# Reordering the first two batches of a fused attention and layer-norm kernel

## What is computed

```
u = einsum('bld,bmd->blm', h, h) / sqrt(d)
p = softmax(u, axis=-1)
delta = p * adjacency
attn = delta / (sum(delta, axis=2) + 1e-10)
h_left, h_self, h_right = h @ W_left.T + b_left, h @ W_self.T + b_self, h @ W_right.T + b_right
attn_left  = where(j > i, attn, 0)      # above the diagonal
attn_right = where(j < i, attn, 0)      # below it
ctx = attn_left @ h_left + diag(attn) * h_self + attn_right @ h_right
o = layernorm(ctx, eps=1e-12) * gamma + beta
x = layernorm(x + relu(o), eps=1e-5)
```

## Times and profile before

| | us |
|---|---|
| median of 3 runs | 479.48 |
| lowest, highest | 479.28, 480.9 |
| the profiled execution | 482.81 |
| its span in the trace | 481.1 |
| PE busy, share | 464.3, 97% |
| DVE busy, share | 360.3, 75% |
| ACT busy, share | 325.8, 68% |
| POOL busy, share | 222.2, 46% |

### The profile page before, as it was taken

The page is one execution under the profiler, slowest core; times in us unless marked ns, Lnnn a source line. Parts: engine busy times, 40 slices in busy tenths (PEclk is TensorE's granted clock), DMA queues, the critical chain, the costliest instruction groups (busy, mean ns, idle before and its releaser), DMA issues.

```text
span 481.1 us, 9627 instructions
## 1 busy us (share of the span) xinstructions
PE 464.3 (97%) x2712; PEld 459.5 (96%) x2712; DVE 360.3 (75%) x1088; ACT 325.8 (68%) x715; POOL 222.2 (46%) x294
## 2 busy tenths in 40 slices
PE   8989799999999999999999999999999999999992
PEld 7979799999999999999999999999999999999982
DVE  5667667887777778877777887777788777777756
ACT  6644666677667667766766776676677667667752
POOL 0104543445554444555444455544445554444552
PEclk8999799999999999999999999999999999999998
DMA  8555465465565644556555455655445566544211
GB/s 254 161 162 186 146 187 190 128 194 181 184 188 185 200 138 163 184 176 198 185 172 159 166 183 170 207 185 173 153 165 185 174 207 185 170 156 134 85 71 65
DMA packets 85350, 81.25 MB, mean 169 GB/s; under 512 B 7250, under 2 KB 77396, under 8 KB 85332
## 3 DMA queue, kind: packets, MB, share of 16 engines
q1 hardware_dynamic: 85328, 81.03, 52.6%
q10 hardware_dynamic: 4, 0.00, 0.0%
HBM read 52.17 MB, written 28.84 MB: 168 GB/s over the span
## 4 chain that ended last, share of the span: by engine, by line
PE 88%; DVE 4%; POOL 3%; issue 2%; ACT 2%; SPq 1%; DMA 0%; POOLq 0%; DVEq 0%
PE ps_proj L454 58%; PE ps_ctx L468 19%; PE ps_scores L433 4%; PE ps_scores L442 4%; POOL rstd L976 1%; PE ps_scores L396 1%; SPq L294 1%; POOL shifted L984 1%; ACT normed L576 1%; POOL scaled L980 1%; ACT ps_scores L527 1%; DVE stats L750 1%; DVE y_sb L783 0%; DMA dt_raw<-dt_dram 0%; PE ps_ctx L403 0%
## 5 line engine op out<-in xcount | busy, mean ns | idle before, releaser
L454 PE MATMUL ps_proj<-w_hi,xt_hi 128*128 128x384 f32 x576 | 197.2, 342 | 5.0 <-ACT ps_proj L546 5.0
L454 PE MATMUL ps_proj<-w_lo,xt_hi 128*128 128x384 f32 x576 | 195.9, 340 | 0.0
L454 PE MATMUL ps_proj<-w_hi,xt_lo 128*128 128x384 f32 x576 | 195.8, 340 | 0.0
L976 POOL TENSOR_TENSOR rstd<-var_eps,minus_half 128x4 f32<-128x4 f32 x32 | 42.9, 1340 | 191.7 <-DVE var_eps L769 189.2
L454 PEld LDWEIGHTS ps_proj<-w_hi,xt_hi 128*128 128x128 f32 x576 | 109.6, 190 | 6.5 <-ACT ps_proj L546 6.5
L454 PEld LDWEIGHTS ps_proj<-w_hi,xt_lo 128*128 128x128 f32 x576 | 109.5, 190 | 0.0
L454 PEld LDWEIGHTS ps_proj<-w_lo,xt_hi 128*128 128x128 f32 x576 | 109.3, 190 | 0.0
L550 ACT ACTIVATE proj_hi<-ps_proj 128x384 fp32r<-128x384 f32 x128 | 63.5, 497 | 58.2 <-PE ps_proj L454 58.1
L546 ACT ACTIVATE ps_proj<-bias 128x384 f32<-128x384 f32 (+1 forms) x192 | 92.9, 497 | 0.9 <-DVE proj_lo L735 0.7
L735 DVE TENSOR_TENSOR proj_lo<-ps_proj,proj_hi 128x384 fp32r<-128x384 f32 x128 | 69.7, 548 | 16.9 <-ACT proj_hi L550 14.9
L980 POOL TENSOR_TENSOR scaled<-normed,gamma_sb 128x384 f32<-128x384 f32 x62 | 63.2, 1020 | 36.8 <-ACT normed L576 32.3
(11 more groups left out here) (89 smaller groups left out, 660.4 us busy)
## 6 DMA issues: line engine op xcount, KB each, us to landing
x_sb<-in_x SPq DMA_DIRECT2D x32, 384.0 KB, 4.3
xt_sb<-in_x_t SPq DMA_DIRECT2D x31, 384.0 KB, 3.8
out_dram<-out_sb SPq DMA_DIRECT2D x31, 384.0 KB, 2.9
adj_sb<-in_adj SPq DMA_DIRECT2D x32, 256.0 KB, 4.4
cross_dram<-cross_turned SPq DMA_DIRECT2D x31, 256.0 KB, 2.0
cross_raw<-cross_dram SPq DMA_DIRECT2D x124, 64.0 KB, 2.0
dt_dram<-turned SPq DMA_DIRECT2D x31, 256.0 KB, 2.0
dt_raw<-dt_dram SPq DMA_DIRECT2D x124, 64.0 KB, 2.0
```

The source lines that it names most:

```text
L454: mm = nc.tensor.matmul(ps_proj[bank(at, g)][:, 0:H], stationary, moving[w][:, c, :], start=False, stop=True, skip_group_check=True)
L976: nc.gpsimd.tensor_tensor(rstd[at.slot(2)][:], var_eps[:], minus_half[:], ALU.pow).then_inc(rstd_ready, 1)
```

## The change

It touches the prologue and batches 0 and 1 only.

- The two bias rows are spread before the first scores, one after the other. The four warm-up transposes are gone, and so is ACT's read of the zeros ahead of its two bias DMAs.
- Batch 0's LEFT and RIGHT groups are projected chunk by chunk for both row tiles (`project_both`), so that a weight chunk serves 6 matmuls as soon as it is there.
- Batch 1's scores are computed in full (`scores_in_full`, 18 matmuls in place of 12). Its turning, its store and its four loads are gone.
- ACT's and DVE's lists for batch 0 and batch 1 are in another order. In batch 1 ACT's `seed_proj(at, 4)` comes ahead of `exps`; DVE's `turn`, `turn_cross` come ahead of the last `split_proj`; `split_xt` for batch 3 moves into batch 1's step.
- SP: weights come in two DMAs each instead of three; the first adjacency comes after x of batch 1; `x_sb[0]` after the store of batch 2's cross.
- POOL's wait for gamma and beta moves to their first use.
- `bias_row` and `ones_row` are allocated last and `first_read` is dropped, so that every tile behind `bias` lies 3,616 bytes lower.

```diff
+    IN_FULL = 2
...
             def load_weight(w):
-                for c in range(C):
-                    sp.dma_start(w_raw[w][:, c, :], w_rows[w][:, c, :]).then_inc(w_loaded[w][c], 16)
+                for i, (c, d) in enumerate(((0, 1), (1, C))):
+                    sp.dma_start(w_raw[w][:, c:d, :], w_rows[w][:, c:d, :]).then_inc(w_loaded[w][i], 16)
...
             load_weight(LEFT)
-            sp.dma_start(adj_sb[0][:], adj_rows[0]).then_inc(adj_loaded[0], 16)
             load_weight(RIGHT)
             load_xt(1, 1)
+            sp.dma_start(adj_sb[0][:], adj_rows[0]).then_inc(adj_loaded[0], 16)
             load_weight(SELF)
...
-            first = Batch(0, 0)
-            store_cross(first.plus(1))
-            sp.dma_start(x_sb[0][:], x_rows[0]).then_inc(x_loaded[0], 16)
-            load_cross(first.plus(1))
...
+            def project_both(at, w):
+                for c in range(C):
+                    pe.wait_ge(w_lo_ready[w], c + 1)
+                    for t in range(T):
+                        g = GROUPS.index((w, t))
+                        if c == 0:
+                            pe.wait_ge(proj_seeded, g + 1)
+                        mm = product(at, g, c)
+                        if c == C - 1:
+                            mm.then_inc(proj_ready, 1)
...
             mm.then_inc(banks_opened, 1)
-            pe.wait_ge(ident_ready, 1)
-            for _ in range(WARM_UP):
-                nc.tensor.transpose(ps_scores[1][:, 0, 0:P], ident[:], ident[:])
             first = Batch(0, 0)
             pe.wait_ge(ones_row_ready, 1)
-            first_scores(first)
+            spread(LEFT)
             spread(RIGHT)
+            scores_in_full(first)
...
+                if at.b == 0:
+                    project_both(at, LEFT)
+                    project_both(at, RIGHT)
+                    first_turn(at)
+                    scores_in_full(nxt)
+                    project(at, 4)
+                    open_context(at)
+                    project(at, 5)
+                    cross(ahead)
+                    attend(at, 0)
+                    attend(at, 1)
+                    return
...
-            act.wait_ge(zeros_ready, 1)
-            nc.scalar.activation(first_read[:], zeros[:, 0:1].bitcast(F32), ACT.Copy)
...
             split_first_xt()
-            for c in range(C):
-                split_weight(LEFT, c)
+            split_weight(LEFT, 0)
             act.wait_ge(banks_opened, 1)
             act.wait_ge(ones_ready, 1)
-            for g in range(2):
-                seed_proj(first, g)
-            exps(first)
-            for c in range(C):
-                split_weight(RIGHT, c)
-            for g in range(2, PBANKS):
-                seed_proj(first, g)
+            seed_proj(first, 0)
+            split_weight(LEFT, 1)
+            seed_proj(first, 1)
+            split_weight(LEFT, 2)
+            split_weight(RIGHT, 0)
+            seed_proj(first, 2)
+            split_weight(RIGHT, 1)
+            seed_proj(first, 3)
+            split_weight(RIGHT, 2)
+            exps(first)
...
-            split_xt(first.plus(3))
...
                 split_proj(at, 0)
+                if at.b == 1:
+                    split_xt(ahead)
                 normalise(before)
                 split_proj(at, 1)
+                if at.b == 1:
+                    seed_proj(at, 4)
                 if nxt.exists(BATCHES):
                     exps(nxt)
-                seed_proj(at, 4)
+                if at.b != 1:
+                    seed_proj(at, 4)
+                if at.b == 1:
+                    seed_proj(at, 5)
+                split_proj(at, 2)
                 if at.b == 1:
                     split_delta(at)
-                split_proj(at, 2)
-                seed_proj(at, 5)
+                else:
+                    seed_proj(at, 5)
...
+            copy_bias(LEFT)
             split_weight(LEFT, 0)
-            copy_bias(LEFT)
+            copy_bias(RIGHT)
+            split_weight(LEFT, 1)
             finish_scores(first)
-            for c in range(1, C):
-                split_weight(LEFT, c)
-            copy_bias(RIGHT)
+            split_weight(LEFT, 2)
+            for c in range(C):
+                split_weight(RIGHT, c)
...
+                if at.b == 1:
+                    diagonal(at)
+                    split_proj(at, 0)
+                    norm_shift(before)
+                    finish_scores(nxt)
+                    split_proj(at, 1)
+                    split_xt(ahead)
+                    deltas(nxt)
+                    split_proj(at, 2)
+                    split_delta(at)
+                    turn(nxt)
+                    turn_cross(ahead)
+                    split_proj(at, 3)
```

More of the change, by code:

```diff
@@ L119, in gnn_resnorm @@
         bias = [sb(f"bias{w}", [P, HE]) for w in range(3)]
-        bias_row = [sb(f"bias_row{w}", [1, H]) for w in (LEFT, RIGHT)]
-        ones_row = sb("ones_row", [1, P])
-        first_read = sb("first_read", [P, 1])
         gamma_sb = sb("gamma_sb", [P, H])
@@ L168, in gnn_resnorm @@
         shifted = sb("shifted", [P, T, H])
+        bias_row = [sb(f"bias_row{w}", [1, H]) for w in (LEFT, RIGHT)]
+        ones_row = sb("ones_row", [1, P])
         ps_scores = [psum(f"ps_scores{i}", [P, T, L]) for i in range(2)]
@@ L182, in gnn_resnorm @@
         first_xt_loaded = [sem(f"first_xt_loaded{c}") for c in range(C - 1)] + [xt_loaded[0]]
-        w_loaded = [[sem(f"w_loaded{w}_{c}") for c in range(C)] for w in range(3)]
+        w_loaded = [[sem(f"w_loaded{w}_{i}") for i in range(2)] for w in range(3)]
         bias_row_loaded = [sem(f"bias_row_loaded{w}") for w in (LEFT, RIGHT)]
@@ L408, in first_turn @@
                 pe.wait_ge(bias_ready, 2)
+                pe.wait_ge(ident_ready, 1)
                 for t in range(T):
@@ L444, in squares, with product @@
                 mm.then_inc(scores_ready, 1)
+            def product(at, g, c):
+                w, t = GROUPS[g]
+                hi, lo = xt(at, c, t * P, (t + 1) * P)
+                for stationary, moving in ((hi, w_hi), (hi, w_lo), (lo, w_hi)):
+                    mm = nc.tensor.matmul(ps_proj[bank(at, g)][:, 0:H], stationary, moving[w][:, c, :], start=False, stop=True,
+                                          skip_group_check=True)
+                return mm
             def project(at, g):
@@ L491, in one @@
                         attend(at, 0)
-                    if at.b == 0 and g == 1:
-                        first_turn(at)
-                    if at.b == 0 and g == 3:
-                        cross(nxt)
-                    if at.b == 0 and g == 4:
-                        open_context(at)
-                    if g == 4 and at.b != 0 and ahead.exists(BATCHES):
+                    if g == 4 and ahead.exists(BATCHES):
                         cross(ahead)
-                if at.b == 0:
-                    squares(nxt)
-                    cross(ahead)
                 if not last(at):
@@ L695, in finish_scores @@
             def finish_scores(at):
-                if at.b != 0:
-                    dve.wait_ge(cross_loaded, at.n(64, 0))
+                in_full = at.b is not None and at.b < IN_FULL
+                if not in_full:
+                    dve.wait_ge(cross_loaded, at.n(64, 64 * (1 - IN_FULL)))
                 dve.wait_ge(scores_ready, at.n(1, 1))
@@ L836, in _ @@
             split_delta(first)
+            split_weight(SELF, 1)
+            split_weight(SELF, 2)
+            split_proj(first, 1)
+            finish_scores(first.plus(1))
             split_xt(first.plus(2))
@@ L839, in _ @@
                 split_proj(first, g)
-            finish_scores(first.plus(1))
             turn_cross(first.plus(2))
@@ L843, in _ @@
             turn(first.plus(1))
-            diagonal(first.plus(1))
-            split_xt(first.plus(3))
             def one(at):
@@ L978, in gamma_of @@
             def gamma_of(at, t):
+                if at.b == 0 and t == 0:
+                    pool.wait_ge(vectors_loaded, 2 * 16)
                 pool.wait_ge(normed_ready, at.n(T, t + 1))
```

86 lines of the change are left out of this document (38 added, 48 removed).

## The result

| | before | changed |
|---|---|---|
| median, us | 479.38 | 471.71 |
| lowest, highest | 477.09, 480.9 (4 runs) | 471.55, 472.5 (4 runs) |
| profiled execution | 482.81 | 471.55 |
| its span | 481.1 | 469.8 |
| PE busy | 464.3, 97% | 456.4, 97% |

The ratio is 0.9846, with a 95% interval of 0.9808 to 0.9884: faster by 7.7 us.

The account below looks back on a forecast made before the run. PE, busy 97% of the span, was taken as the bound, with time to gain only up to the fourth batch. Gains of 1.6 + 2.1 + 4.6 = 8.3 us from the profiled 482.81 gave 474.5; forecast 474.2, range 471.0 to 477.5.

Parts of the forecast that it names:

- The start: Stretch up to the squares of batch 2: they start at 25.9 instead of 27.48, a gain of 1.6 us.
- I let the clock rise the same 3.4 us after the scores begin: Start: low clock lasts 3.4 us into the scores, so projecting starts at 9.6 against 8.95, 0.65 us lost.
- Batch 1: Stretch of 16.60 us between squares: costs 14.5 with a 0.4 wait for the triangles, a gain of 2.1 us.
- the new order puts the seed ahead of the exponentials: Batch 1: new order and scores finished 6 us earlier remove PE's wait of 1.90 us for a seed.
- Batch 2: Stretch of 20.08 us between squares: costs 15.5 with a 1.4 wait for a seed, a gain of 4.6 us.
- from 64.16 on I let everything stay and shift: Everything from 64.16 us, the third batch mark, to the end: unchanged, only shifted, so no gain there.
- Rival D: Addresses: tiles behind `bias` move 3,616 bytes; 1 ns more per matmul costs 2.7 us, less gains; 480 us, chance 0.04.
- The 3.3 us: Profiled execution above the median: either usual for profiled executions (471.2) or batch 2's bad luck (474.5), the second much likelier.
- The Trainium skill's rule on transposes: Start: transposes don't count as PE activity, so the clock rises at 7.9, 0.6 us less, total 473.6.
- A: Rival, start: the low clock lasts, the rise as late as 12.5; costs up to 1.5 us, 476 us, chance 0.16.
- B: Rival: batch 2 stays late through slow load issue, wait about 3 us and clock falls; 477.5 to 479, chance 0.17.
- C: Rival: slower, as a wait for batch 1's late triangles replaces the removed one; 482 us, chance 0.05.

Follow-up runs that it names:

- run 2: Changed kernel with an unused 3,616-byte tile behind the biases, so all tiles lie where they lay before: 475.35 us, ratio 0.9925.
- run 6: Kernel before with only batch 1's scores computed in full, dropping its trip through DRAM; head, orders and tile places as before: 476.33 us against 478.76, ratio 0.9935.
- run 7: Changed kernel with ACT's and DVE's lists of batch 1 put back in the old order: 472.06 us, ratio 0.9852.
- run 1: Kernel before with only bias_row, ones_row and first_read allocated last, tiles behind the biases 3,616 bytes lower: 475.71 us against 479.06, ratio 0.994.
- run 11: Kernel before with PE's new head alone: spreads first, no warm-up transposes, no ACT read of the zeros: 479.83 us against 479.03, ratio 1.0027.

## Why the prediction was right, and where it wasn't

The number was right for a mixture of reasons, and in part by luck. Without the new places the change measures 475.35 (run 2), 3.7 below the kernel before, where 5.3 was forecast. The places, which the sum held at nothing, give the other 3.6.

**The start** (forecast gain 1.6, here 1.9). The spreads took 1.43 each against 1.5, scores began at 5.84 against 6.0, and projecting at 9.34 against 9.6. The step "I let the clock rise the same 3.4 us after the scores begin" gave a single number to what is a spread of numbers. In the ten traces whose scores start at 5.84 with the spreads in front, full pace (the first matmul whose distance to the next is the full one) comes at 8.75, 8.99, 9.58, and in the other seven between 11.07 and 11.98. The changed kernel's trace was the luckiest of them: the squares of batch 2 start at 25.58 there and at 26.6 to 27.0 in the late ones that have its lists for the head. By medians the head may be worth about 1 us: run 6 (476.33) and run 2 (475.35) differ by the head and the orders alone, and run 7 gives the orders nothing clear of the noise. The intervals of runs 6 and 2 overlap, so this 1 us isn't shown.

**Batch 1** (forecast 14.5, here 14.78). The wait for the triangles, 0.4, was right. But "the new order puts the seed ahead of the exponentials, and finishes batch 1's scores 6 us earlier" named two causes, and only the second counts: without the order the wait for the seed is 0.17 (run 7).

**Batch 2** (forecast 15.5, here 15.94). In the changed kernel the path is the one that was forecast: the delta is in at 43.26, ahead of the variances at 44.35 (44.2 forecast), DVE's list is the limit, and the wait of 1.4 came as 1.71, with the clock at 1.00. What the gain was given to was wrong. I gave it to the cross that is turned ahead of the residual and to what follows from it; with all orders as before, batch 2 takes 15.43 and 15.49 (runs 7 and 6). What made 20.08 of it was the slow issue and the low clock behind the wait. I had counted the slow issue as happening "once in the whole trace"; the trace of before has three of over 2.5 us (3.85, 2.67 at 131.24 and 2.61 at 453.75), and the nine kernels with the new orders have one in batch 2 as well, where the earlier loads hide it.

**The rest** ("from 64.16 on I let everything stay and shift"). This is the step that failed, by 3.4 us. Rival D had the place (all tiles behind `bias` move), the scale (1 ns for each matmul is 2.7 us) and the sign to watch ("less is a gain"), but its chance was given to a loss alone. "Against it, the projections' slices in use lie 1,544 bytes apart and their matmuls all go at one pace" looked at the context's operands; the pair that matters is weights and x's halves. No row read from the trace of before tells the price, and a kernel with that one edit (run 1) does.

**The 3.3 us** between the profiled execution and the median. I took it for the luck of one execution. That fits: 482.81 - 8.3 = 474.5 describes the changed kernel without the new places, and run 2 measures 475.35; the other reading, 471.2, is 4.2 away from it. The luck has a wider source than batch 2, though. In run 1's trace the clock fell behind the wait of 1.87 in batch 1, the like of which I had read as one that "left the clock at 1.00":

```profile
34.00:37.00 3.00, 1.13 (x7) 0.81 (x6) 1.35 (x6) 3.00 (x10) 0.00 (x0) 1.00 0.79 231
37.60:40.60 3.00, 3.00 (x13) 3.00 (x13) 2.43 (x6) 2.09 (x6) 2.77 (x6) 0.50 1.07 362
```

These are stretches of run 1: the first holds the wait, the second stands at a granted 0.50. Batch 1 takes 17.88 there instead of 16.60, and with the 0.12 of the places that is 1.4 us more. So a wait near 1.9 may or may not take the clock with it: the two others of 1.90, in the kernel before and in run 11, did not. This may be part of why the runs of before spread over 3.8 to 6.5 us; one execution of each kernel was traced, so it isn't shown. The changed kernel keeps a wait of 1.71 in batch 2. In its trace and in six of its variants, with 1.61 to 1.70, the clock stayed up behind it.

**The Trainium skill's rule on transposes** ("TensorE: Matmul & The Clock Gate", "Part 4: PE-mode transpose") can't be decided here: the rise comes so unevenly that 8.75 speaks neither for 7.9 nor for 9.4. Behind transposes the rise came 1.8 us after the first score in the kernel before, sooner than in any of the ten traces without them (2.9 at least). But runs 1 and 6 have the same transposes in front, and there the first twelve scores all stand at the low pace, 2.5 us long. In run 6 the last six, up to 9.71, do as well. The Trainium skill says on the same page, in "Part 1: The HAM clock gate", that the rise varies from run to run with where the first matmul happens to fall. The traces agree that it varies, and by more than the half microsecond to either side that the Trainium skill gives there: 2.9 to 6.1 us behind the first score, with the same instructions in front. Had I used that sentence, the start would have had a range in place of a number.

Of the rivals, A came half true (the rise often comes near 11.5, and the squares of batch 2 then start 1.1 to 1.4 us later). B's slow issue came (2.42 in the changed kernel), but neither its wait of 3 us nor the low clock. C did not come, and D came with the other sign.

## What to carry to other kernels

When a change touches the allocation, compare the distance of the same matmuls in a steady stretch before and after, to the thousandth: 2 ns in each of 1,728 projecting matmuls is near half of the gain here. Put the moving and the stationary operand of a pair at different places within 64 bytes and measure it, since it costs a pad of 32 bytes. Before a gain is given to a new order, run the structural part (here the dropped trip through DRAM) without it. And before a gain is given to that part, compare stretch by stretch what came earlier: in batch 2 it was the length of one issue.

## What the runs showed that I had not expected

- The projecting matmuls of 384 columns take 0.1736 us if their two operands lie at different places within 64 bytes and 0.1756 to 0.1760 if they lie alike. Those of 386 columns (3.16 against 3.17 for 18) hardly change. The Trainium skill's page "TensorE: Matmul & The Clock Gate", "Part 2: What happens when you issue a matmul", has the stationary operand loaded through a read port of its own, so that it takes nothing from the running matmul. Here the places of the two do bear on each other, by 1.2 to 1.4% (7.90 and 7.92 against 7.81); the measurement decides.
- The granted clock in the records reads 1.00 at the start although matmuls stand at the low pace. From 6.00 to 8.50 us after the change, 12 matmuls of 256 columns fit, 0.21 apart, where 0.12 is full pace:

```profile
6.00:8.50 2.50, 2.50 (x12) 2.50 (x13) 1.06 (x2) 1.58 (x5) 0.00 (x0) 1.00 1.02 354
```

There the distance of the matmuls is to be read, not the clock's column.
- Two matmuls of a single row keep PE busy from 2.99 to 5.84 and bring no rise: in none of the ten traces that have them in front did it come less than 2.9 us behind the first score.
